# First expert stage in 64-slot units on quarters of the array; in both expert stages the last two units reach the tokens by one-hot products

## The chip, the cores and the metric

The kernel runs on one core of one Trainium2 chip. The metric is the device time of one execution in microseconds (us). The kernel before was run three times beside this work; the times were 405.24, 405.71 and 405.87, median 405.71.

## The reference, cut to what is computed

The input is 16 images of 96 x 96 pixels. A patch embedding (five shifted copies of each 16 x 16 patch, layer norm, linear map) gives 16 x 36 = 576 tokens of 192 numbers. Then follow an attention block with 12 heads and rounded operands, a first mixture of experts, a state-space block with a gated feed-forward part, and a second mixture of experts. Only the two mixtures of experts are changed.

```
# first mixture: 8 experts, the best one per token, hidden width 512
for e in range(8):
    mask = (max_ind == e)[:, None]
    xe = where(mask, x, 0)
    oe = silu(xe @ w1[e]) * (xe @ w2[e]) @ w3[e]
    out = out + where(mask, oe, 0)
out = out.astype(bfloat16) * max_prob          # then added to the residual stream

# second mixture: 8 experts, the best two per token, hidden width 768
# y = sum over the two experts of gate * (silu(x @ Wg[e].T) * (x @ Wu[e].T)) @ Wd[e].T
```

Everything is float32 except where the kernel names bf16.

## The kernel before, in words

576 tokens lie in SBUF as five tiles of 128 rows (`TT` = 5, the last has 64), 192 columns wide.

**Routing.** `experts(m, tile)` on DVE (m = 0 and 1 for the two mixtures) takes the largest logits, ranks each token within its expert, and gives each token and choice a slot. Slots are cut into units of 128 (`P`), each with one expert: units 0 to 7 are the first 128 slots of experts 0 to 7, the units from 8 on hold what is over. There are `M1_TILES` = 12 units in the first mixture and `M2_TILES` = 16 in the second, whatever the routing is. `src_id` (L1166) names the token of each slot, `row_id` (L1169) the DRAM row to which a slot's result goes.

**Data flow of a unit.** SP loads the expert's weights (`expert_weights`, L417 to L421: `wup` in four transfers, `wdn` in one) into one of 8 buffers (first mixture) or 6 (second). POOL gathers the unit's token rows from DRAM (`gather`, L597); for unit 0 PE does it by a product with a one-hot matrix (`first_tile`, L1547). PE transposes the rows (`gathered`, L1580), ACT and DVE copy them to `xgt` (L770, L1190). PE multiplies gate and up weights with the tokens: `up_main` (L1604) with the first 128 of 192 input rows on the whole array, `up_rest` (L1616) with the last 64, gate on rows 0 to 63 of the array and up on rows 64 to 127 at the same time. ACT takes silu (L774), DVE the product (L1196) to `ht`. PE multiplies by the down weights (`down`, L1629), ACT copies the result to `ysb` (L781), and POOL scatters it to the DRAM scratch `token_y` (L604). After the last unit SP waits for all scatters (`results`, L445) and loads `token_y` in token order to `yg` (L349). DVE adds gate times `yg` to the residual `h` (`routed`, L1211, in the first mixture; L1332 in the second, after which the tiles of `h` go out).

**Order.** Every engine's order is written out by hand. On PE, unit j is `up_main(j, 0)`, `up_main(j, 1)`, a transposition of a later unit, `up_rest(j, 0)`, `up_rest(j, 1)`, `down(j - 1)`. All weights go through SP's one queue, in program order: six loads of the first mixture after the embedding (`v_h` = 5), then the writes of the token rows (`token_rows`, L349), loads 6 and 7, loads from 8 on as buffers come free (`later_experts` waits for `p_y`, the count of finished `down`), then `results(0)`, then the first load of the second mixture. The loads of experts 0 to 7 of the first mixture have constant addresses, later ones take the expert's number from `te`.

**Layout of the weights in DRAM.** For the first mixture `w12` is, for each expert, 96 rows x 2 halves x 1024 columns (512 gate, 512 up) in float32; `w3` is 128 rows x 4 x 192. A unit's weights are 1.18 MB.

Of the kernel before, what the change touches and what calls it, by code (L numbers as in the profile page):

```python
# [50 lines left out]
M1_TILES = (T + E * (P - 1)) // P  # L51
# [5 lines left out]
W_LOADS = 5  # L57
AHEAD = 4
MAMBA_AT, ATTENTION_AT = 23 * 1024, 56 * 1024
# [38 lines left out]
def build(nc, A, out):  # L98

    with ExitStack() as ctx:  # L100
# [96 lines left out]
        slot_m = sb("slot_m", [P, 2, TT])  # L197
        slot_r = sb("slot_r", [P, 2, TT])
# [10 lines left out]
        def weight_buffers(m, n, hid):  # L209
# [60 lines left out]
        ysb = [sb("ysb0", [P, 2, D], BF16, scope=arena), sb("ysb1", [P, 2, D], scope=arena)]  # L270
        yg = [sb("yg0", [P, 1, TT, D], BF16, scope=arena), sb("yg1", [P, 2, TT, D], scope=arena)]
        xg = sb("xg", [P, M2_TILES, DW], scope=arena)
        xgt = sb("xgt", [P, 2, M2_TILES * P], scope=arena)
        one_first = sb("one_first", [P, TT, P], scope=arena)
        arena.close()
# [28 lines left out]
            d_gam d_x0 d_x0b d_w0b d_wub d_x1 d_x2 d_w0 d_w1 d_w2 d_wu d_att d_ssm d_tx d_out  # L304
# [5 lines left out]
            v_x2 v_fc v_cs v_f0 v_first v_val  # L310
            a_sq a_xp a_s12 a_std a_xt a_rx a_qf a_vf a_at a_of a_ot a_ex a_gt a_sg a_y a_cp a_z a_xs a_dt
            a_dec a_ysq a_fc a_f1
            p_ch p_st p_ht p_tr p_rt p_qk p_v p_sc p_av p_otr p_proj p_lg p_rk p_inv p_gt p_gu p_y p_in p_dt p_g
            p_seg p_xs p_ys p_ssq p_out p_fc p_f2""".split()}
        d_y = (S["d_ya"], S["d_yb"])
        MOE = (dict(n=M1_TILES, hid=M1_H, k=1, w12=A["m1_w12"], w3=A["m1_w3"], before=0, bufs=M1_BUFS),
               dict(n=M2_TILES, hid=M2_H, k=2, w12=A["m2_w12"], w3=A["m2_w3"], before=M1_TILES, bufs=M2_BUFS))
        for r in MOE:
            r["groups"] = [(0, 1), (1, 2)] + [(i, i + 2) for i in range(2, r["n"], 2)]
            r["group_of"] = [i for i, (lo, hi) in enumerate(r["groups"]) for _ in range(lo, hi)]  # L320
# [3 lines left out]
        def weight_uses(m, j):  # L324

            b = j % MOE[m]["bufs"]
            uses = j // MOE[m]["bufs"] + 1
            if m == 1:
                uses += len(range(b, M1_TILES, M1_BUFS))
            return b, uses  # L330

        def rows_gathered(m, i):
# [6 lines left out]
            return 16 * rows  # L339

# [6 lines left out]
        def _(sp):  # L347
# [56 lines left out]
            def expert_weights(m, j, e=None):  # L404
# [4 lines left out]
                b, _ = weight_uses(m, j)  # L409
# [7 lines left out]
                sp.dma_start(up[0:DH, 0:2 * hid], w12[:, 0, :]).then_inc(S[f"d_wb{b}"], 16)  # L417
                sp.dma_start(up[DH:P, 0:2 * hid], w12[0:lo, 1, :]).then_inc(S[f"d_wb{b}"], 16)
                sp.dma_start(up[0:REM, 2 * hid:3 * hid], w12[lo:DH, 1, 0:hid]).then_inc(S[f"d_wb{b}"], 16)
                sp.dma_start(up[REM:P, 2 * hid:3 * hid], w12[lo:DH, 1, hid:2 * hid]).then_inc(S[f"d_wb{b}"], 16)  # L420
# [31 lines left out]
            sp.wait_ge(S["v_h"], TT)  # L452
            for j in range(6):
                expert_weights(0, j)
# [20 lines left out]
            for t in range(TT):  # L475
                rows = P if t < TT - 1 else LAST
                sp.wait_ge(S["v_h"], 5 * TT + t + 1)
# [5 lines left out]
        def _(pool):  # L483
# [105 lines left out]
            def experts_io(m):  # L589
# [12 lines left out]
                def scatter(j):  # L602
                    pool.wait_ge(S["a_y"], j + 1 + before)
# [7 lines left out]
                for j in range(n):  # L611
# [3 lines left out]
                    if j >= 1:  # L615
                        scatter(j - 1)
                scatter(n - 1)
# [30 lines left out]
        def _(act):  # L648
# [94 lines left out]
            def experts(m):  # L743
# [22 lines left out]
                def gathered(i):  # L766

                    lo, hi = r["groups"][i]
                    act.wait_ge(S["p_gt"], 2 * (GROUPS[m] + i) + 1)
                    a.copy(xgt[:, 0, lo * P:hi * P], ps[:, 6, 0:(hi - lo) * P]).then_inc(S["a_gt"], 1)  # L770
# [5 lines left out]
                def result(j):  # L776

                    act.wait_ge(S["p_y"], j + (1 + before))
                    if j >= 2:
                        act.wait_ge(d_y[j % 2], j // 2 * 16 + 8 * before)  # L780
# [1064 lines left out]
```

## Time and profile before

| | |
|---|---|
| median of the runs | 405.71 us |
| profiled execution, its own time | 409.78 us |
| its span | 408.0 us |
| PE busy | 348.6 us (85%) |
| DVE, ACT, POOL busy | 184.0, 134.8, 104.5 us |
| moved by the DMA engines | 59.51 MB, mean 146 GB/s |

The span is the time from the first to the last instruction of the program in the profiled execution; its own time has some 1.8 us around it. A busy share is over the whole span. In the tables below a "x16" counts recorded instructions: a float32 product of the program is two MATMUL records (and two weight loads), a bf16 one is one. Times on the left are microseconds from the start of the span.

### The profile page before, as it was taken

How to read it: one execution, taken by the hardware profiler on the slowest of the kernel's cores; microseconds unless marked ns; L12 is line 12 of the kernel's file. 1: busy time of each engine (PE TensorE's matmuls, PEld its weight loads, DVE VectorE, ACT ScalarE, POOL GpSimd, SP SyncE). 2: the span in 40 equal slices, each digit the busy share in tenths (PEclk: the TensorE clock that was granted, in tenths of full speed). 3: DMA queues.
4: the chain of work that ended last, by engine and by line, in shares of the span. 5: the costliest groups of instructions: out<-in, count | busy, mean ns of one | idle time of the engine just before them, and what ended most of it. 6: DMA issues, size and time to landing. Idle time of an engine off the chain costs nothing.

```text
span 408.0 us, 7081 instructions
## 1 busy us (share of the span) xinstructions
PE 348.6 (85%) x2758; PEld 291.5 (71%) x2758; DVE 184.0 (45%) x474; ACT 134.8 (33%) x278; POOL 104.5 (26%) x133
## 2 busy tenths in 40 slices
PE   4999946989788999966896987888899999999970
PEld 1999923567667999962465654575799999999960
DVE  2786793996552222216398555266422212121213
ACT  2997311444303222321387042321321212121210
POOL 3299542000023443122032202000423232211120
PEclk9999976987776999996999798995999999999995
DMA  7933239930371795007003999002249999999204
GB/s 237 345 84 75 63 81 253 271 93 2 108 202 52 203 247 124 15 16 195 0 0 77 258 252 259 28 0 67 60 105 291 277 254 255 258 251 249 65 31 130
DMA packets 28707, 59.51 MB, mean 146 GB/s; under 512 B 10081, under 2 KB 15234, under 8 KB 28674
## 3 DMA queue, kind: packets, MB, share of 16 engines
q1 hardware_dynamic: 26274, 53.48, 50.1%
q0 software_dynamic: 2400, 5.57, 5.0%
q8 instruction: 22, 0.36, 0.4%
q14 instruction: 11, 0.09, 0.1%
HBM read 55.12 MB, written 3.92 MB: 145 GB/s over the span
## 4 chain that ended last, share of the span: by engine, by line
PE 60%; DVE 17%; ACT 8%; DMA 8%; issue 4%; SPq 2%; POOL 0%; DVEq 0%; POOLq 0%; ACTq 0%
PE ps L1604 15%; PE ps L1629 12%; PE ps L1616 9%; PE ps L1412 4%; PE ps L1345 4%; DMA xw<-in_xw 3%; DVE cv L1264 3%; ACT xp L661 2%; PE ps L1418 2%; DVE xn L974 2%; DVE xn L950 2%; PE ps L1467 2%; SPq L349 2%; PE ps L1547 2%; DMA yg<-token_y 2%
## 5 line engine op out<-in xcount | busy, mean ns | idle before, releaser
L1604 PE MATMUL ps<-xgt,wup 128*128 128x128 f32 x576 | 70.9, 280 | 2.3 <-DVE ht L1196 1.8
L1604 PEld LDWEIGHTS ps<-xgt,wup 128*128 128x128 f32 x576 | 69.4, 196 | 2.8 <-issue 2.8
L1196 DVE TENSOR_TENSOR ht<-sg,ps 128x384 f32<-128x384 f32 (+1 forms) x56 | 27.7, 497 | 77.5 <-ACT sg L774 75.5
L597 POOL DMA_INDIRECT xg<-token_x,src_id x26 | 25.3, 972 | 145.5 <-DVE src_id L1166 95.3
L1629 PE MATMUL ps<-wdn,ht 128*128 128x192 f32 x288 | 53.8, 335 | 0.0
L1345 PE MATMUL ps<-busy 128*128 128x512 bf16 x108 | 38.9, 486 | 11.1 <-DVE h L1211 6.6
L1629 PEld LDWEIGHTS ps<-wdn,ht 128*128 128x128 f32 x288 | 46.1, 190 | 3.1
L604 POOL DMA_INDIRECT token_y<-ysb,row_id x28 | 27.5, 981 | 67.6 <-ACT ysb L781 67.6
L774 ACT ACTIVATE sg<-ps 128x384 f32<-128x384 f32 (+1 forms) x56 | 24.8, 444 | 49.9 <-PE ps L1616 49.1
L1353 PE MATMUL ps<-weff,xp 128*128 128x193 f32 x240 | 39.9, 327 | 1.6 <-ACT xp L661 1.6
L1353 PEld LDWEIGHTS ps<-weff,xp 128*128 128x128 f32 x240 | 39.2, 190 | 2.4 <-issue 2.4
L1616 PE MATMUL ps<-xgt,wup 64*128 64x128 f32 x576 | 40.5, 286 | 0.0
L1616 PEld LDWEIGHTS ps<-xgt,wup 64*128 64x128 f32 x576 | 35.0, 190 | 4.2 <-issue 2.5
L1190 DVE COPY xgt<-ps 128x256 f32<-128x256 f32 (+1 forms) x14 | 5.7, 405 | 49.2 <-PE ps L1580 49.2
L1345 PEld LDWEIGHTS ps<-busy 128*128 128x128 bf16 x108 | 11.9, 116 | 22.2 <-issue 8.3
L661 ACT COPY xp<-xw 128x576 f32<-128x576 f32 x24 | 16.0, 667 | 6.7 <-DMA xw<-in_xw 6.7
L770 ACT COPY xgt<-ps 128x256 f32<-128x256 f32 (+1 forms) x14 | 5.0, 357 | 38.4 <-PE ps L1580 38.4
L1388 PE MATMUL ps<-ident,xn 128*128 128x128 f32 x30 | 6.3, 301 | 10.9 <-DVE xn L950 8.9
L690 ACT ACTIVATE std<-mv,eps_t 128x1 f32<-128x1 f32 x20 | 5.9, 294 | 28.4 <-DVE mv L960 28.4
L1388 PEld LDWEIGHTS ps<-ident,xn 128*128 128x128 f32 x30 | 3.9, 149 | 15.0 <-DVE xn L950 10.6
L781 ACT COPY ysb<-ps 128x192 f32<-128x192 f32 x16 | 5.1, 318 | 26.3 <-PE ps L1629 26.3
L909 DVE TENSOR_REDUCE acc<-wall 128x192 f32<-128x3072 f32 (+1 forms) x2 | 10.5, 5236 | 5.3 <-ACT wall L674 3.8
(295 smaller groups left out, 511.0 us busy)
## 6 DMA issues: line engine op xcount, KB each, us to landing
wup<-in_m_w SPq DMA_DIRECT2D x16, 576.0 KB, 8.5
wup<-in_m_w SPq DMA_DIRECT2D x48, 192.0 KB, 9.4
wdn<-in_m_w SPq DMA_DIRECT2D x16, 576.0 KB, 11.4
wup<-in_m_w SPq DMA_DIRECT2D x12, 384.0 KB, 6.1
wup<-in_m_w SPq DMA_DIRECT2D x36, 128.0 KB, 6.6
wdn<-in_m_w SPq DMA_DIRECT2D x12, 384.0 KB, 9.3
xw<-in_xw SPq DMA_DIRECT2D x2, 784.0 KB, 12.3
wall<-in_w_sh SPq DMA_DIRECT2D x2, 768.0 KB, 10.2
```

The costliest lines, as they stand in the source:

```text
L597: g.indirect_dma_start(xg[:, j, :], None, token_x[m], bass.IndirectOffsetOnAxis(ap=src_id[:, j:j + 1], axis=0))\
L604: g.indirect_dma_start(token_y[m], bass.IndirectOffsetOnAxis(ap=row_id[:, j:j + 1], axis=0), ysb[m][:, j % 2, :], None).then_inc(d_y[j % 2 ...
L661: a.copy(xp[:, n % RING, 0:T].rearrange("p (b r x) -> p b r x", r=GRID, x=GRID), img[:, :, wy:wy + GRID, wx:wx + GRID]).then_inc(S["a_xp"], 1)
L774: a.activation(sg[:, s, 0:half], ps[:, 2 * s, 0:half], ACT.Silu).then_inc(S["a_sg"], 1)
L1196: v.tensor_tensor(ht[:, j % 2, s, 0:half], sg[:, s, 0:half], ps[:, 2 * s + 1, 0:half], ALU.mult)\
L1264: v.scalar_tensor_tensor(out=cv[:, r], in0=xpad[:, r, :, k:k + NTOK], scalar=convw[:, r, k:k + 1], in1=cv[:, r], op0=ALU.mult, op1=ALU.add ...
L1345: mm(ps[:, bank, :], busy[:, 0:P], busy[:], start=True, stop=True)
L1353: return mm(ps[:, TILE_BANK[t], 0:D + 1], xp[:, n % RING, t * P:t * P + P], weff[:, n, 0:D + 1], start=(n == 0), stop=(n == NCH - 1))
L1412: mm(outs[v][b], w[:, 0, c0:c1], moving(v, b), start=True, stop=False)
L1604: mm(ps[:, 2 * s + g, c * P:c * P + P], up[:, col:col + P], xgt[:, 0, j * P:j * P + P], start=(c == 0), stop=False)
L1616: ins = mm(ps[:, 2 * s + g, c * P:c * P + P], up[rows, col:col + P], xgt[rows, 1, j * P:j * P + P], start=False, stop=(c == tiles - 1))
L1629: ins = mm(ps[:, 4 + j % 2, 0:D], ht[:, j % 2, c // tiles, c % tiles * P:c % tiles * P + P], dn[:, c, :], start=(c == 0), stop=(c == 2 * t ...
```

## The change

**Units of 64 slots.** In the first mixture slots are cut into units of 64 (`H`): 16 of them (`M1_HALVES`), two by two in 8 pairs (`M1_TILES` = 8). Each half has its own expert and so its own weights. A pair is gathered by one indirect transfer as before. The 192 input rows are now three blocks of 64 (`KB` = 3), and each product is done on a quarter of the array: 64 rows x 64 columns of it, gate on rows 0 to 63, up on rows 64 to 127, and two column halves i. `across`, `up_half` and `down_pair` take the place of `gathered`, `up_main`/`up_rest` and `down`. The pair's result is the sum of two PSUM banks: ACT copies one to `y_low`, DVE adds the other (`both_rows`). On PE the order is `up_half(j, 0)`, `down_pair(j - 1)`, `across(j + 1)`, `up_half(j, 1)`.

**Weight layout and loads.** `wup` holds for each block k both the gate rows (partitions 0 to 63) and the up rows (64 to 127), 512 columns each. A load is seven transfers instead of five: blocks 0 and 2 by one transfer each, whose destination is 128 partitions x 512 and whose source is 2 (gate, up) x 64 rows x 512; block 1 by four of 32 rows; and `wdn`. There are 16 loads instead of 12.

**The last two units.** In both mixtures the last two units (`KEPT` = 2) are not scattered. `token_y` is filled with zeros by three transfers on SP ahead of the first weight load. DVE makes one-hot matrices, tokens x slots, for the two units (`last_units`, after units 2 and 3, and 4 and 9; in the second mixture they carry the gates), PE transposes them (`kept_across`) with the last units, ACT and DVE copy them out, and after the last `down` PE adds one-hot times result for each token tile (`combine`). In the first mixture `combine` also takes `yg` through an identity product and DVE's `routed` reads PSUM; in the second, DVE adds the PSUM tile to `h` after both `yg` parts. `results` waits for the scatters of the other units alone.

```diff
-M1_TILES = (T + E * (P - 1)) // P
+H = 64
+M1_HALVES = (T + E * (H - 1)) // H
+M1_TILES = (M1_HALVES + 1) // 2
+KB = D // H
-W_LOADS = 5
+W_LOADS = (7, 5)
+KEPT = 2
...
+        KEPT_AFTER = ((2, 3), (4, 9))
...  SP: expert_weights
+                if m == 0:
+                    def both(k):
+                        return up[:, k * hid:(k + 1) * hid]
+
+                    def gate_and_up(half, rows):
+                        return w12[rows, half, :].rearrange("p (g n) -> g p n", g=2)
+
+                    pieces = [(both(0), gate_and_up(0, slice(0, H))), (both(2), gate_and_up(1, slice(lo, DH)))]
+                    for g in range(2):
+                        at = H * g
+                        pieces += [(up[at:at + DH - H, hid:2 * hid], w12[H:DH, 0, g * hid:(g + 1) * hid]),
+                                   (up[at + DH - H:at + H, hid:2 * hid], w12[0:lo, 1, g * hid:(g + 1) * hid])]
...
+                for dst, src in pieces:
+                    sp.dma_start(dst, src).then_inc(S[f"d_wb{b}"], 16)
                 sp.dma_start(down[:], w3).then_inc(S[f"d_wb{b}"], 16)
...  SP: later_experts
-                for j in range(first, r["n"]):
+                for j in range(first, M1_HALVES if m == 0 else r["n"]):
                     if j == E:
                         sp.wait_ge(S["v_te"], m + 1)
-                    sp.wait_ge(S["p_y"], j - r["bufs"] + 1 + r["before"])
+                    last = j - r["bufs"]
+                    sp.wait_ge(S["p_y"], (last // 2 if m == 0 else last) + 1 + r["before"])
...  SP: results
-                    sp.wait_ge(d_y[b], 8 * (r["n"] + r["before"]))
+                    sp.wait_ge(d_y[b], 8 * (r["n"] - KEPT) + scattered(m))
...  SP, after v_h = 5
+            zeros = (busy[:, 0:D], busy[:].bitcast(F32)[:, 0:D])
+            for m in range(2):
+                for k in range(MOE[m]["k"]):
+                    y = token_y[m][k * TPAD:(k + 1) * TPAD, :].rearrange("(t p) d -> p t d", p=P)
+                    load(y, zeros[m].unsqueeze(1).broadcast_to([P, TT, D]), "d_zero")
...  POOL: experts_io
-                    if j >= 1:
+                    if j == 0:
+                        pool.wait_ge(S["d_zero"], 48)
+                    elif j <= n - KEPT:
                         scatter(j - 1)
-                scatter(n - 1)
...  DVE: last_units(l), both_rows(j)
+                    v.tensor_tensor(ysb[m][:, j % 2, :], y_low[:], ps[:, 5, 0:D], ALU.add).then_inc(S["v_y"], 1)
...
+                    for k in range(K):
+                        for t in range(TT):
+                            ...
+                                ins = v.tensor_scalar(one_last[m][:, l, k, t, :], pos_r[:], slot_k[:, l, k, t:t + 1],
+                                                      gate[:, k, t:t + 1], ALU.is_equal, ALU.mult)
...  PE: first_tile
+                        if m_ == 0:
+                            for c in range(KB):
+                                for i in range(2):
+                                    ins = mm(ps[H * i:H * i + H, 6, c * P:c * P + P], xn[0:k, t, H * c:H * c + H],
+                                             one_first[0:k, t, :], start=(t == 0 and c == 0),
+                                             stop=(t == TT - 1 and c == KB - 1))
...  PE
+                def across(j):
+                    ...
+                    for c in range(KB):
+                        for s in range(2):
+                            rows = slice(H * s, H * s + H)
+                            for i in range(2):
+                                ins = mm(ps[H * i:H * i + H, 6 + s, c * H:c * H + H], xg[rows, j, H * c:H * c + H],
+                                         ident[rows, rows], start=True, stop=True)
+                def up_half(j, s):
+                    ...
+                    for c in range(hid // P):
+                        for k in range(KB):
+                            for g in range(2):
+                                rows = slice(H * g, H * g + H)
+                                for i in range(2):
+                                    col = c * P + H * i
+                                    ins = mm(ps[H * i:H * i + H, 2 * s + g, c * H:c * H + H], up[rows, k, col:col + H],
+                                             xh[rows, t, k, :], start=(k == 0), stop=(k == KB - 1))
+                def down_pair(j):
+                    ...
+                    for c in range(hid // P):
+                        for g in range(2):
+                            rows = slice(H * g, H * g + H)
+                            for i in range(2):
+                                dn = wbuf[0][(2 * j + i) % M1_BUFS][1]
+                                ins = mm(ps[H * i:H * i + H, 4 + g, 0:D], ht[rows, j % 2, i, c * H:c * H + H],
+                                         dn[rows, c, :], start=(c == 0), stop=(c == hid // P - 1))
+                def kept_across(l):
+                    ...
+                    for t in range(TT):
+                        ...
+                        ins = nc.tensor.transpose(at, one_last[1][0:k, l, 0, t, :], ident[0:k, 0:k])
+                def combine():
+                    pe.wait_ge(S["a_oh"], 1 if m_ == 0 else 1 + KEPT)
+                    pe.wait_ge(S["v_oh2"], 1 if m_ == 0 else 1 + KEPT)
+                    pe.wait_ge(S["v_y" if m_ == 0 else "a_y"], n)
+                    if m_ == 0:
+                        pe.wait_ge(S["d_yg"], 32)
+                    for t in range(TT):
+                        k = P if t < TT - 1 else LAST
+                        o = ps[0:k, TILE_BANK[t], 0:D]
+                        if m_ == 0:
+                            mm(o, identb[0:k, 0:k], yg[0][0:k, 0, t, :], start=True, stop=False)
+                        for l in range(KEPT):
+                            ins = mm(o, kept_at[m_][:, l, t * P:t * P + k], ysb[m_][:, (n - KEPT + l) % 2, :],
+                                     start=(m_ == 1 and l == 0), stop=(l == KEPT - 1))
+                        ins.then_inc(S["p_cmb"], 1)
```

## Rows read from the trace of the kernel before

**Rows 1.** The page's chain that ended last: shares of the span by line.
```profile
PE ps L1604 15%; PE ps L1629 12%; PE ps L1616 9%; PE ps L1412 4%; PE ps L1345 4%; DMA xw<-in_xw 3%; DVE cv L1264 3%; ACT xp L661 2%; PE ps L1418 2%; DVE xn L974 2%; DVE xn L950 2%; PE ps L1467 2%; SPq L349 2%; PE ps L1547 2%; DMA yg<-token_y 2%
```
**Rows 2.** The chain in order of time, first mixture: start us, us, what.
```profile
114.69 3.75 PE ps L1547 x20
...
119.51 3.75 DMA xg<-token_x,src_id
...
126.24 3.75 PE ps L1604 x16
129.99 0.85 PE ps L1580 x4
130.84 1.09 PE ps L1616 x16
131.94 1.50 PE ps L1629 x8
133.43 1.78 PE ps L1604 x16
...
177.42 2.81 PE ps L1629 x16
```
**Rows 3.** Timeline, end of the first mixture: start us, us, engine line op, tiles, shapes, count.
```profile
180.25 0.32 ACT L781 CAST ysb<-ps 128x192 bf16<-128x192 f32 x1 [0.98 <-PE ps L1629]
180.84 0.97 POOL L604 DMA_INDIRECT token_y<-ysb,row_id  x1 [0.33 <-ACT ysb L781]
183.12 0.96 SPq L349 DMA_DIRECT2D yg<-token_y  x2
186.35 0.42 DVE L1211 SCALAR_TENSOR_TENSOR h<-yg,gate,h 128x192 f32<-128x192 bf16 x1 [8.05 <-DMA yg<-token_y]
```
**Rows 4.** Stretches: window us; length; busy us (instructions) by engine; PEclk; DMA share; GB/s.
```profile
9.00:16.00 7.00, 6.40 (x39) 6.43 (x40) 4.93 (x6) 7.00 (x14) 0.00 (x0) 1.00 1.03 426
60.00:86.00 26.00, 19.07 (x122) 11.35 (x123) 18.62 (x33) 6.53 (x8) 3.89 (x5) 0.82 1.00 252
126.20:129.90 3.70, 3.66 (x17) 3.69 (x18) 0.29 (x1) 0.00 (x0) 0.94 (x1) 0.50 0.12 35
135.00:157.00 22.00, 22.00 (x203) 20.70 (x203) 5.05 (x12) 6.17 (x17) 9.08 (x11) 1.00 0.99 246
```
**Rows 5.** SP's queue: the first transfer of all, first and last of a later load.
```profile
56.77 0.33 SPq L417 DMA_DIRECT2D wup<-in_m_w  x1
...
134.52 0.34 SPq L417 DMA_DIRECT2D wup<-in_m_w  x1
...
136.94 0.45 SPq L421 DMA_DIRECT2D wdn<-in_m_w  x1
```
**Rows 6.** Groups of instructions by shape: busy us, mean ns of one, idle us before.
```profile
L774 ACT ACTIVATE sg<-ps 128x256 f32<-128x256 f32 x24 | 9.2, 383 | 16.2 <-PE ps L1616 15.4
L1196 DVE TENSOR_TENSOR ht<-sg,ps 128x256 f32<-128x256 f32 x24 | 10.1, 420 | 26.2 <-ACT sg L774 25.9
L1140 DVE TENSOR_SCALAR one_first<-pos_r,slotf 128x128 f32<-128x128 bf16 x10 | 2.1, 281 | 0.1
L1321 DVE TENSOR_TENSOR h<-ps,hb 128x192 f32<-128x192 f32 x5 | 1.7, 340 | 1.4 <-PE ps L1759 1.4
```
**Rows 7.** Timeline, products on two column halves in the state-space block.
```profile
231.11 1.35 PE L1712 MATMUL ps<-mix,dtx 128*64 128x72 f32 x36
```
**Rows 8.** Timeline, end of the kernel.
```profile
390.73 4.17 PE L1629 MATMUL ps<-wdn,ht 128*128 128x192 f32 x24
394.94 0.32 ACT L781 COPY ysb<-ps 128x192 f32<-128x192 f32 x1 [1.63 <-PE ps L1629]
...
397.92 2.15 SPq L349 DMA_DIRECT2D yg<-token_y  x4
403.43 1.73 DVE L1332 SCALAR_TENSOR_TENSOR h<-yg,gate,h 128x192 f32<-128x192 f32 x5 [0.36 <-DMA yg<-token_y]
403.88 2.37 SPq L349 DMA_DIRECT2D out_h<-h  x5
```

More of the change, by code:

```diff
@@ L322, in build, with weight_loads @@
         RESTS = [0, len(MOE[0]["groups"]) - 1]
-        def weight_uses(m, j):
+        def weight_loads(m, j):
             b = j % MOE[m]["bufs"]
-            uses = j // MOE[m]["bufs"] + 1
+            loads = W_LOADS[m] * (j // MOE[m]["bufs"] + 1)
             if m == 1:
-                uses += len(range(b, M1_TILES, M1_BUFS))
-            return b, uses
+                loads += W_LOADS[0] * len(range(b, M1_HALVES, M1_BUFS))
+            return b, 16 * loads
         def rows_gathered(m, i):
@@ L339, in rows_gathered, with scattered @@
             return 16 * rows
+        def scattered(m):
+            return 8 * (M1_TILES - KEPT) if m == 1 else 0
         N_ATT, N_SSM, N_FIRST = 16 * 26, 16 * 40, 14
@@ L602, in scatter @@
                 def scatter(j):
-                    pool.wait_ge(S["a_y"], j + 1 + before)
+                    pool.wait_ge(S["v_y" if m == 0 else "a_y"], j + 1)
                     g.indirect_dma_start(
@@ L778, in result @@
                     act.wait_ge(S["p_y"], j + (1 + before))
+                    if m == 0:
+                        if j >= 1:
+                            act.wait_ge(S["v_y"], j)
+                        a.copy(y_low[:], ps[:, 4, 0:D]).then_inc(S["a_yh"], 1)
+                        return
                     if j >= 2:
-                        act.wait_ge(d_y[j % 2], j // 2 * 16 + 8 * before)
+                        act.wait_ge(d_y[j % 2], j // 2 * 16 + scattered(m))
                     a.copy(ysb[m][:, j % 2, :], ps[:, 4 + j % 2, 0:D]).then_inc(S["a_y"], 1)
@@ L1076, in experts @@
                 r = MOE[m]
-                n, half, before, K = r["n"], r["hid"] // 2, r["before"], r["k"]
+                n, half, before, K, L = r["n"], r["hid"] // 2, r["before"], r["k"], r["slots"]
+                over = (M1_HALVES if m == 0 else n) - E
                 i_ln = 2 if m == 0 else 5
@@ L1334, in _ @@
                                            op0=ALU.mult, op1=ALU.add).then_inc(S["v_h"], 1)
+            for t in range(TT):
+                rows = P if t < TT - 1 else LAST
+                dve.wait_ge(S["p_cmb"], TT + t + 1)
+                dve.wait_ge(S["v_h"], 5 * TT + t + 1)
+                v.tensor_tensor(h[0:rows, t, :], h[0:rows, t, :], ps[0:rows, TILE_BANK[t], 0:D], ALU.add)\
+                    .then_inc(S["v_h"], 1)
         @block.tensor
@@ new lines, in down_pair @@
+                def down_pair(j):
+                    pe.wait_ge(S["v_ht"], 2 * j + 2)
+                    if j >= 1:
+                        pe.wait_ge(S["a_yh"], j)
+                        pe.wait_ge(S["v_y"], j)
+                    else:
+                        pe.wait_ge(S["v_id"], 1)
+                    for c in range(hid // P):
+                        for g in range(2):
+                            rows = slice(H * g, H * g + H)
+                            for i in range(2):
+                                dn = wbuf[0][(2 * j + i) % M1_BUFS][1]
+                                ins = mm(ps[H * i:H * i + H, 4 + g, 0:D], ht[rows, j % 2, i, c * H:c * H + H],
+                                         dn[rows, c, :], start=(c == 0), stop=(c == hid // P - 1))
+                    ins.then_inc(S["p_y"], 1)
@@ new lines, in experts @@
+                if m_ == 0:
+                    for j in range(n):
+                        up_half(j, 0)
+                        if j >= 1:
+                            down_pair(j - 1)
+                        if j + 1 < n:
+                            across(j + 1)
+                        else:
+                            for l in range(KEPT):
+                                kept_across(l)
+                        up_half(j, 1)
+                    down_pair(n - 1)
+                    combine()
+                    return
@@ L1644, in experts @@
                 down(n - 1)
+                combine()
             experts(0)
```

196 lines of the change are left out of this document (153 added, 43 removed).

## The prediction

> **What bounds the kernel now.** I read the page's chain first, then the same chain in order of time, then the stretches with their DMA rate. Matmuls of the two mixtures of experts are the three longest entries of the chain [rows 1]: there PE waits for nothing, and what is taken off it is time won, as long as nothing else is late. In the first mixture a unit of 128 slots costs PE 1.78 us (16 records, L1604) + 1.09 (L1616) + 1.50 (L1629), and 0.85/2 or less for the transpositions (0.85 at half clock), some 4.6 us in all [rows 2]. Twelve of them end at 180.2. Then comes a tail without PE: copy (180.25), scatter (180.84), load of `yg` (183.12), and DVE's first add at 186.35 [rows 3]. The same tail stands at the end: ACT copies at 394.94, DVE's last add ends at 405.16, the last store is issued by 406.25 and the span ends at 408.0 [rows 8]. The weights are hidden today, but not by much: from 135 to 157 four loads keep the DMA engines 0.99 busy at 246 GB/s [rows 4].
>
> **PE's work in the first mixture.** An `up_half` has 4 x 3 x 2 x 2 = 48 products, 96 records, four quarters at a time: 24 rounds of 64 columns. A record of 128 columns takes 1.78/16 = 0.111 us at full clock and 3.75/16 = 0.234 at half [rows 2], where the granted clock is 0.50, 1.2 GHz [rows 4]; for 64 columns half of that. So an `up_half` is 1.3 us, or 2.8 at half clock. `down_pair` has 8 rounds of 192 columns at 1.50/8 = 0.19: 1.5 us (3.0). `across` is 6 rounds: 0.3. A pair costs 2 x 1.3 + 1.5 + 0.3 = 4.5 us, eight of them 36 where twelve units took 55. That four quarters run together no row shows. Two row halves do: 16 records of 128 columns in 1.09 us, 0.068 each instead of 0.111 [rows 2]. Two column halves do: 36 records of 72 columns in 1.35 us, 0.037 each, where one after the other would have 0.111 x 72/128 = 0.062 [rows 7]. The bounds for a pair are 4.5 us and, with two quarters at a time, 9.
>
> A rule of the Trainium skill speaks against this: a matmul with few columns costs as much as one with 60, the overhead is paid per instruction (TensorEngine Tiling (Array Packing), Performance Considerations, Instruction Overhead). By it, in an estimate of mine with its 60 cycles at 2.4 GHz, 25 ns, for each of a pair's 216 records of 64 columns, a pair would be 5.4 + 1.5 = 6.9 us. The row with two column halves stays above that at 37 ns, so it can't refute it; the sum below doesn't change by it, since weights are later than that.
>
> **The beginning.** `first_tile` has 60 records, 30 rounds, instead of 20 (3.75 us, L1547): +1.8 us before the first gather, 119.5 becomes 121.3 [rows 2]. No wait of later units hangs on it if the loads set the pace.
>
> **The loads.** This is the term that decides. A load has 1.18 MB, as before; 16 instead of 12. SP issues seven transfers instead of five; five take 134.52 to 137.39, 0.58 us each [rows 5], so seven 4.1 us: no bound below. The two large ones (262,144 bytes each) have a destination of 128 rows and a source of 2 x 64 rows. All large transfers of the kernel before have 96, 32, 64 or 128 rows outermost on both sides, all multiples of 16, so the trace doesn't show what an outermost 2 does. The bounds: over all 16 engines at 252 GB/s [rows 4] such a piece is 1.0 us; over two engines each has 131,072 bytes. One engine moves 252/16 = 15.8 GB/s when all are busy, 426/16 = 26.6 at best [rows 4]: 8.3 to 4.9 us a piece. I take two engines. The work has to be dealt out along a dimension that both sides count, and the outermost ones are 128 and 2; nothing else of the two matches. The Trainium skill says it outright: the number of engines is the largest up to 16 that divides the outermost dimension of both sides (DMA: Bandwidth & Descriptors, Why a DMA increments its semaphore by 16 and not by 1). No row here shows it; by it the piece has two engines.
>
> The two busy engines then carry for each load 2 x 131,072 bytes and 1/16 of the other 655,360: 303,104 bytes. Of the rate I take 24 GB/s, near the upper row, since fourteen engines are idle beside them, and below it for rows of 2 KB: 12.6 us a load. In order of the queue: SP starts at 56.8 [rows 5]. The zeros are 1.23 MB, 4.9 us at 252 GB/s: 61.7. Sixteen loads: 202 us. Token rows, gathers and scatters are 1.9 MB, their share of the two engines 117,000 bytes, 4.9 us. With 1 us to land the last load is there at 269.6. The queue is never empty between: loads 0 to 7 last until 61.7 + 101 = 163, and load 8 waits only for the first `down_pair`. That comes late too: the token rows stand behind loads 0 to 5 on the same engines (61.7 + 76 = 137), so the first gather lands at 142 instead of 123, and the first pair is done by 152.
>
> **The tail of the first mixture.** PE has idled for most of 12 us before each half, so I count half clock: last `up_half` 2.8, silu and product 0.38 + 0.42 [rows 6] with 0.1 of handing over, `down_pair` 3.0, copy to `y_low` 0.32 [rows 3], sum 0.35, handing over 0.2, three bf16 products and handing over 0.8: 8.4 us (5.3 at full clock). `yg` is issued after the sixth scatter, stands behind the loads in the queue and lands 1 us after the last: hidden. `routed(0)` starts at 278.0, not 186.35: +91.7 us. One-hot matrices of DVE (5 x 0.28 and a few small ones, 1.6 us twice) lie in that waiting. What follows is DVE's chain as before, so it moves along rigidly; the first load of the second mixture is early.
>
> **The second mixture.** PE gets ten float32 transpositions with units 14 and 15: 20 records at 0.11, +2.2 us, no cover. DVE's `last_units` is 10 x 0.28 + 0.9 + 0.2 = 3.9 us after units 4 and 9; DVE is busy 1.2 us of a unit's 6.4, and its next product is asked for some 5 us later: hidden; without that cover up to 2 x 2.7. The tail after the last `down` (394.90) is now: copy 0.35, then `combine`, 20 records at 0.17 (4.17/24 [rows 8]) and handing over, 3.6, last add 0.34 [rows 6], then issue, landing and end, 2.84 as before (408.0 - 405.16): 7.1 instead of 13.1, less 0.4 because PE's pace spreads the five stores: 6.7. The 14th scatter is issued before `down(14)`, its load of `yg` (2.15 + 3.4 us) and the ten adds are done 1 us before `combine` needs DVE. So -6.4 + 2.2 = -4.2 us. Bounds: 0 if `yg` is late by a unit, -6.
>
> **Sum.** In the profiled execution: 409.78 + 91.7 - 4.2 = 497.3 (span 495.5). That execution was 4.1 us above the median of the runs; from the median: 405.7 + 87.5 = 493.2.
>
> **Rivals.** *A. The two pieces are spread over 16 engines.* For it: every other transfer is. Then two loads, a gather and a scatter, 2.54 MB, take 10.3 us at 246 GB/s [rows 4], more than PE's 4.5, so the loads bound pairs 4 to 7. The first `down_pair` ends near 132 (before 133.4, [rows 2]), load 8 starts at 134.1, eight are there at 175.4, the tail is 5.3 to 8.4: `routed(0)` at 182.3, -4.1. Time 405.7 - 4.1 - 4.2 = 397.4. Faster: this is the case of the other sign. *B. Sixteen engines, but quarters don't overlap fourfold.* A pair costs 9 us; eight from 122 on (half an `up_half` runs before the first gather is there at 124) and a tail of 5 end at 199, +12.7 - 4.2: 414. The first mixture gets slower from 7.4 us a pair, (186.35 - 5 - 122)/8, the kernel from 7.9. Against it: both halvings overlap. *C. Two engines, and slow ones*, at the 15.8 GB/s of a full queue: a load 19.2 us, +105: 599. Against it: that rate was shared by sixteen. *D. Two engines at 26.6 GB/s*: 11.4 us, -19: 474.
>
> **Numbers.** Two engines 0.79 (C at its end 0.03, D beside the forecast), A 0.15, B 0.04, else 0.02. The likeliest case alone has 465 to 545. For the range I go to A, as without it 0.2 would be left: 394 to 545. About 0.2% (0.8 us) is what a measurement of this kernel can tell from no change. Faster: A but for a little of it, 0.15. Same 0.02. Slower: two engines and B, 0.83.
>
> **What would show it.** Landing of the first pieces: 5 us or more apart and DMA busy share near 0.13 to 0.2 through the first mixture, PE idle before `up_half` on `wup`, one load every 12 to 13 us. `combine` without `yg` on its wait. Clock 0.50 in the last halves. The prediction is wrong if the DMA share is near 1.0 there and loads come every 5 us; then A holds.

## The result, and the profile after

The changed kernel takes 493.62 us (median of 4 runs, 492.27 to 494.69) against 405.79 us for the kernel before (4 runs); the ratio is 1.2153, with a 95% interval of 1.2105 to 1.2202. The forecast was 493.2. The profiled execution took 494.69 us and has a span of 493.0.

The page of the kernel after, first the slices, then the chain by engine and by line (its line numbers are the changed kernel's: L454 issues the pieces of the first weights, L455 the second weights, L1803 is `up_half`, L1822 `down_pair`, L1779 `across`, L1864 the one-hot products):

```profile
PE   6999388976026742323252888788879999999996
DMA  7832332232433323233227000799010399999703
...
PE 39%; SPq 26%; DMA 10%; DVE 10%; ACT 5%; issue 5%; POOL 4%; DVEq 0%; ACTq 0%; POOLq 0%
SPq L454 24%; PE ps L1739 8%; PE ps L1764 7%; DMA wdn<-in_m_w 6%; PE ps L1751 5%; PE ps L1803 4%; DVE cv L1385 3%; PE ps L1539 2%; DMA token_x<-xn 2%; PE ps L1822 2%; DMA xg<-token_x,src_id 2%; DVE xn L1042 1%; PE ps L1472 1%; PE ps L1965 1%; PE ps L1545 1%
...
L1803 PE MATMUL ps<-xgt,wup 64*64 64x64 f32 x1536 | 38.8, 281 | 69.8 <-DMA wdn<-in_m_w 66.8
```

Where [rows 1] had matmuls of the two mixtures on top, SP's queue now has 24% of the span, and `up_half` has waited 66.8 us for weights. The chain in order of time (start, us, what) shows one load of SP's queue, then the first pair of units:

```profile
90.67 0.54 SPq L454
91.25 3.95 SPq L454
95.25 5.06 SPq L454
100.35 0.42 SPq L454
...
101.74 0.42 SPq L455
102.21 0.54 SPq L454
...
127.58 9.82 DMA token_x<-xn
...
138.27 6.39 DMA xg<-token_x,src_id
144.71 0.92 PE ps L1779 x24
145.63 4.04 PE ps L1803 x192
149.66 1.50 PE ps L1822 x29
...
151.94 1.51 PE ps L1803 x102
153.45 1.90 issue
155.35 1.54 PE ps L1803 x89
```

From 90.67 to 102.21 is one load. Its plain transfers are issued in 0.42 us each; each of the two large pieces keeps a place in SP's queue for 4 to 5 us. What the DMA engines do meanwhile stands in three stretches (window; length; busy us of PE, PEld, DVE, ACT, POOL; PEclk; DMA share; GB/s); in the first a large piece is alone under way:

```profile
70.50:75.00 4.50, 4.50 (x33) 3.60 (x32) 3.61 (x9) 1.43 (x2) 0.00 (x0) 1.00 0.13 51
64.00:126.00 62.00, 49.52 (x583) 35.69 (x583) 37.16 (x130) 19.80 (x35) 0.00 (x0) 0.86 0.29 97
156.00:256.00 100.00, 38.33 (x1316) 35.78 (x1312) 9.67 (x33) 7.39 (x21) 6.28 (x7) 0.63 0.31 101
```

A share of 0.13 is 2.1 of 16 engines, so two engines at 51/2 = 25.5 GB/s each; [rows 4] had 0.99 and 246 GB/s. The last load and the tail, beside [rows 3]:

```profile
256.44 11.01 DMA wdn<-in_m_w
267.45 0.04 issue
267.49 2.88 PE ps L1803 x96
...
270.81 0.43 DVE ht L1269
...
271.28 1.57 PE ps L1822 x32
...
273.84 0.24 PE ps L1862
...
274.29 0.43 DVE h L1332
```

The first add of the first mixture is at 274.29 instead of 186.35: +87.9 us. From there to the end of the span it is 218.7 us instead of 221.7, in these two executions. The end of the kernel, beside [rows 8], in the timeline:

```profile
485.55 0.32 ACT L830 COPY ysb<-ps 128x192 f32<-128x192 f32 x1 [1.63 <-PE ps L1764]
486.01 3.63 PE L1864 MATMUL ps<-ysb,kept 128*128 128x192 f32 x20 [0.50 <-ACT ysb L830]
487.45 3.13 SPq L368 DMA_DIRECT2D out_h<-h  x5
489.69 0.35 DVE L1460 TENSOR_TENSOR h<-h,ps 64x192 f32<-64x192 f32 x1 [0.44 <-PE ps L1864]
```

The loads of `yg` are off this path. From the last copy to the end of the span it is 7.5 us, where before it was 408.0 - 394.94 = 13.1.

### The profile page after: what moved, and what is told of

It reads as the page before. It is cut to its first block, busy times and chain, and to the rows that moved or that the text cites. A ratio compares the mean times of both kernels' runs of the same rounds, so it can differ in the third digit from the quotient of the medians.

```text
span 493.0 us, 10359 instructions
## 1 busy us (share of the span) xinstructions
PE 349.3 (71%) x4311; PEld 291.4 (59%) x4311; DVE 194.6 (39%) x519; ACT 132.1 (27%) x269; POOL 93.2 (19%) x121
## 4 chain that ended last, share of the span: by engine, by line
PE 39%; SPq 26%; DMA 10%; DVE 10%; ACT 5%; issue 5%; POOL 4%; DVEq 0%; ACTq 0%; POOLq 0%
SPq L454 24%; PE ps L1739 8%; PE ps L1764 7%; DMA wdn<-in_m_w 6%; PE ps L1751 5%; PE ps L1803 4%; DVE cv L1385 3%; PE ps L1539 2%; DMA token_x<-xn 2%; PE ps L1822 2%; DMA xg<-token_x,src_id 2%; DVE xn L1042 1%; PE ps L1472 1%; PE ps L1965 1%; PE ps L1545 1%
## 5 line engine op out<-in xcount | busy, mean ns | idle before, releaser
L1803 PE MATMUL ps<-xgt,wup 64*64 64x64 f32 x1536 | 38.8, 281 | 69.8 <-DMA wdn<-in_m_w 66.8
L1269 DVE TENSOR_TENSOR ht<-sg,ps 128x384 f32<-128x384 f32 (+1 forms) x48 | 24.4, 509 | 140.6 <-ACT sg L818 138.9
L1803 PEld LDWEIGHTS ps<-xgt,wup 64*64 64x64 f32 x1536 | 36.5, 192 | 71.4 <-DMA wdn<-in_m_w 68.0
L1739 PE MATMUL ps<-xgt,wup 128*128 128x128 f32 x384 | 45.6, 275 | 1.2 <-DVE ht L1269 1.2
L1739 PEld LDWEIGHTS ps<-xgt,wup 128*128 128x128 f32 x384 | 44.8, 192 | 1.4 <-issue 1.4
L644 POOL DMA_INDIRECT token_y<-ysb,row_id x20 | 19.7, 986 | 102.0 <-DVE ysb L1277 63.6
L1764 PE MATMUL ps<-wdn,ht 128*128 128x192 f32 x192 | 35.2, 334 | 0.0
L1764 PEld LDWEIGHTS ps<-wdn,ht 128*128 128x128 f32 x192 | 30.8, 190 | 1.8
L1751 PE MATMUL ps<-xgt,wup 64*128 64x128 f32 x384 | 25.8, 280 | 0.0
L1779 PE MATMUL ps<-ident,xg 64*64 64x64 f32 x168 | 4.5, 234 | 28.4 <-DMA xg<-token_x,src_id 25.6
L1751 PEld LDWEIGHTS ps<-xgt,wup 64*128 64x128 f32 x384 | 22.8, 188 | 2.1 <-issue 1.3
L1779 PEld LDWEIGHTS ps<-ident,xg 64*64 64x64 f32 x168 | 4.2, 146 | 29.2 <-DMA xg<-token_x,src_id 25.7
L1822 PE MATMUL ps<-wdn,ht 64*64 64x192 f32 x256 | 15.6, 390 | 1.0 <-DVE ht L1269 1.0
```

The source lines that it names most:

```text
L644: g.indirect_dma_start(token_y[m], bass.IndirectOffsetOnAxis(ap=row_id[:, j:j + 1], axis=0), ysb[m][:, j % 2, :], None).then_inc(d_y[j % 2 ...
L1269: v.tensor_tensor(ht[:, j % 2, s, 0:half], sg[:, s, 0:half], ps[:, 2 * s + 1, 0:half], ALU.mult)\
L1739: mm(ps[:, 2 * s + g, c * P:c * P + P], up[:, col:col + P], xgt[:, 0, j * P:j * P + P], start=(c == 0), stop=False)
L1751: ins = mm(ps[:, 2 * s + g, c * P:c * P + P], up[rows, col:col + P], xgt[rows, 1, j * P:j * P + P], start=False, stop=(c == tiles - 1))
L1764: ins = mm(ps[:, 4 + j % 2, 0:D], ht[:, j % 2, c // tiles, c % tiles * P:c % tiles * P + P], dn[:, c, :], start=(c == 0), stop=(c == 2 * t ...
L1803: ins = mm(ps[H * i:H * i + H, 2 * s + g, c * H:c * H + H], up[rows, k, col:col + H], xh[rows, t, k, :], start=(k == 0), stop=(k == KB - 1))
```

## The experiments

Times are medians, to be compared with the kernel before on the same chip: 405.8 us for e1 to e4, 405.5 for e5 to e8, 406.9 for e9 to e11. "2 outermost" says that the slowest dimension of a transfer's source has two entries (gate, up), each of 64 rows. "Issue" in a row of waits is time in which an engine stood still and nothing in the profile released it.

**e1_plain: the two pieces as four transfers of 64 rows.**

```diff
-pieces = [(both(0), gate_and_up(0, slice(0, H))), (both(2), gate_and_up(1, slice(lo, DH)))]
+for k, half, rows in ((0, 0, slice(0, H)), (2, 1, slice(lo, DH))):
+    for g in range(2):
+        pieces.append((both(k)[H * g:H * g + H], w12[rows, half, g * hid:(g + 1) * hid]))
```

> Edit: each of the two large pieces of a load goes as two transfers of 64 rows (gate columns, up columns), nine transfers a load, same bytes, everything else as in the changed kernel. Theory T (a piece whose source has 2 outermost and whose destination has 128 rows runs on two DMA engines, and the busier engines' bytes, 303,104 a load at 24.6 GB/s, set 12.3 us a load): now all transfers have 32 or 64 rows on both sides, 1.18 MB a load over sixteen engines, 4.8 us at 246 GB/s; the first add of the first mixture near 182, second mixture 3.0 us shorter than before as measured, time 405.8 - 4.1 - 3.0 = 399 (397 to 402; nine issues of 0.46 us each are 4.1 us a load and set nothing). Rival S (what costs is the issuing of many rows by SP, 4.6 to 5.1 us for a piece of 128 rows, whatever the engines): 128 rows of 2 KB are still issued per piece, so a load keeps its 12.3 us and the time stays at 494.

Measured: 411.8 us (409.99 to 419.35), ratio to before 1.0155 (1.004 to 1.027). The same bytes into the same places, and 82 us are gone: rival S falls. But 399 was expected; 12.8 us are missing. The waits of PE from 118 to 192 us (us in total, times, longest), then SP's timeline (start, us):

```profile
PE ps L1806 <- issue: 10.2, 6, 2.4
PE ps L1806 <- DMA wdn<-in_m_w: 7.9, 3, 4.1
PE ps L1782 <- issue: 5.3, 4, 2.0
```
```profile
155.68 5.10 SPq L457 DMA_DIRECT2D wup<-in_m_w  x8
160.96 0.35 SPq L458 DMA_DIRECT2D wdn<-in_m_w  x1
162.08 1.28 SPq L457 DMA_DIRECT2D wup<-in_m_w  x2
```

Two things show. A load whose address comes from a register takes 162.08 - 155.68 = 6.4 us on SP with nine transfers, more than the 4.8 us in which its data would move at 246 GB/s [rows 4]: SP sets the pace of loads 8 to 15. And PE stands still for 15.5 us ("issue") with nothing to release it. e5_five and the runs behind it part these.

**e2_half: only the second piece in plain transfers.** The edit is that of e1_plain for `both(2)` alone.

> Edit: only the second large piece of a load goes as two transfers of 64 rows; the first stays in one with 2 outermost. Theory T: the busier engines carry 131,072 + 917,504/16 = 188,416 bytes a load, at 24.6 GB/s 7.7 us; sixteen loads are 16 x 4.6 = 74 us shorter, time 420. A half dose gives a little more than half the effect left, 14 us above the kernel before. Rival S, a hold of 5 us for each transfer with 2 outermost whatever its bytes: 5 + 7 x 0.46 = 8.2 us a load, 428. Rival S by rows: 494.

Measured: 432.2 us (2 runs), ratio 1.066 (1.0535 to 1.0785). Loads with fixed addresses came 8.4 us apart (7.7 expected), the one piece held SP 4.7 us. The time is 12 us over T's sum, as in e1_plain. The dose shows, but this run alone doesn't choose between T and a hold of 5 us for each such transfer: that rival's 8.2 us a load and 428 are the nearer numbers. The next run chooses.

**e3_cols: each piece in two column halves, still 2 outermost.**

```diff
+pieces.append((both(k)[:, at], gate_and_up(half, rows)[:, :, at]))   # at: 256 of 512 columns
```

> Edit: both large pieces keep 2 outermost in the source, but each goes as two transfers of half the columns (128 rows of 1 KB): nine transfers, same bytes on the same two engines, twice the number of rows. Theory T: 12.3 us a load as before, 494, and up to 510 if rows of 1 KB move at less than 24.6 GB/s on an engine; each SP issue is held about 2.5 us instead of 5. Rival S (5 us for each such transfer or for each 128 rows): 4 x 5 + 5 x 0.46 = 22.3 us a load, 16 x 10 = 160 us more, 654.

Measured: 496.3 us (2 runs). Twice the transfers and rows, 2.6 us of SP's queue each, 12.7 us a load. The hold goes with the bytes, not with the number of transfers or rows. That leaves no form of S: 654 was its time here. A stretch with one such piece alone:

```profile
73.00:75.00 2.00, 2.00 (x16) 1.47 (x14) 1.97 (x5) 0.20 (x1) 0.00 (x0) 1.00 0.13 48
```

**e4_four: the same pieces with 4 outermost.**

```diff
+return w12[REM // 2 * k:REM // 2 * (k + 1)].rearrange("p m (g n) -> (m g) p n", g=2)
```

> Edit: the same seven transfers and bytes, but the two large pieces read with 4 outermost (32 rows of w12 each) instead of 2; the rows then stand in another order, so that the first mixture computes with other weights. Theory T: four engines carry a piece, 2 x 65,536 + 655,360/16 = 172,032 bytes a load on the busiest, 7.0 us; 16 x 5.3 = 85 us less than the changed kernel, time 409, and the busy share of the DMA engines while one piece is alone under way is 0.25 instead of 0.13. Rival: any piece whose two sides differ in their outermost number runs on two engines, or is held 5 us at issue whatever the number: 494.

Measured: 423.1 us (2 runs), loads 7.3 us apart (7.0 expected), 2.4 us of SP's queue for a piece, and with one alone under way:

```profile
71.40:73.70 2.30, 2.30 (x18) 1.85 (x17) 2.26 (x6) 0.57 (x1) 0.00 (x0) 1.00 0.26 102
```

Twice the share and twice the rate of 2 outermost. In both cases, with 128 on the other side, the number of engines is the outermost number of the source. The time is 14 us over a sum that knows only bytes.

**e5_five: a load in five transfers.**

```diff
+chunks = up.rearrange("p (k n) -> p k n", k=KB)
+pieces.append((chunks[at:at + H // 2], w12[:, i, g * hid:(g + 1) * hid].rearrange("(p k) n -> p k n", k=KB)))
+# the tokens' columns to match: x.rearrange("r (n k) -> r k n", k=KB)[:, c]
```

> Edit: a load in five transfers (gate and up columns, each in two of 32 rows x 3 chunks x 2 KB, and the second weights), for which the three chunks of the contraction take every third row of w12 and every third column of the tokens; same bytes, products and instructions of PE. In the run with nine plain transfers SP took 6.7 us for a load whose address comes from a register, and was never waiting after 129 us, and PE stood still for 15.5 us between 118 and 192 in ten stretches that nothing in the profile releases, each beside a fetch of 16 KB of PE's own instructions. Theory F (PE's instructions are supplied no faster than one such block of 256 in 4.3 us; a pair has 248 matmuls and as many weight loads, 496, so 8.3 to 8.5 us): SP's load falls to 4.4 us, but the pairs keep their 8.5 us; the first down_pair ends at 128, the eighth at 187.6, the first add 189, time 405.8 + 2.9 - 3.0 = 406 (403 to 408). Rival P (only SP's issues held the pairs; PE needs its 5.0 us busy a pair): loads of 5.15 us set the end, first add 177 to 184, time 394 to 400.

Measured: 420.5 us (418.31 to 423.44), ratio 1.0371 (1.0303 to 1.0438). Both theories missed, on the high side, and the kernel is slower than e1_plain, although SP needs less time for a load. PE stood still ("issue") for 26 us and never waited for weights. Its timeline, and two stretches of this run:

```profile
155.81 3.08 PE L1803 MATMUL ps<-xgt,wup 64*64 64x64 f32 x110
164.20 2.10 PE L1803 MATMUL ps<-xgt,wup 64*64 64x64 f32 x69 [5.31 <-issue]
```
```profile
150.00:166.00 16.00, 7.98 (x240) 7.59 (x236) 2.54 (x10) 1.38 (x4) 0.99 (x1) 0.71 1.06 230
182.00:197.00 15.00, 10.74 (x495) 10.10 (x490) 2.51 (x7) 2.73 (x8) 1.94 (x2) 0.95 0.09 22
```

With the DMA engines full PE runs 476 instructions (matmuls and weight loads) in 16 us, with the engines nearly idle 985 in 15; it stands still for 8.0 us of the first stretch and 4.3 of the second. The trace's queue for instructions moves 16 KB at a time. While weights were moved such packets started at 145.62, 152.54, 161.40, 170.12 and 176.54, 6.4 to 8.9 us apart; from 182.03 to 196.78, with the engines nearly idle, 3.4 to 3.9 us apart. The page counts 34 such packets here and 22 in the kernel before:

```profile
q8 instruction: 34, 0.56, 0.6%
```

So theory F's pace, one block in 4.3 us whatever the transfers, is wrong. What it says PE waits for is tested by e7_wide, e9_light and e10_third. The Trainium skill says that crossing such a block is "mostly hidden" (Runtime: NRT & Kernel Launch, Instruction fetch mechanics); in this stage of 64-column products the trace disagrees: PE stood still for 15.5 us in e1_plain and 26 us here.

Waiting isn't what makes this run slower than e1_plain. Between the ends of the first and the eighth `down_pair`, e1_plain (first row) and this run (second):

```profile
128.00:190.00 62.00, 37.64 (x1627) 34.60 (x1625) 12.34 (x39) 9.78 (x27) 7.88 (x8) 0.92 0.64 185
136.00:203.70 67.70, 43.90 (x1622) 40.74 (x1616) 12.18 (x39) 9.76 (x27) 7.88 (x8) 0.85 0.75 175
```

PE stood still for 24.4 and 23.8 us, about the same (in e1_plain 7.9 of it for weights). The 5.7 us between them are PE's work, 43.9 us for 37.6, at a mean granted clock of 0.85 for 0.92. The other 8 us by which the first add is later (205.14 for 191.55) lie before the first `down_pair` ends; what caused them no run shows.

**e6_rows: 64 rows x 128 columns as the stationary.**

```diff
-for i in range(2):
-    ins = mm(ps[H * i:H * i + H, 2 * s + g, c * H:c * H + H], up[rows, k, col:col + H], ...)
+ins = mm(ps[:, 2 * s + g, c * H:c * H + H], up[rows, k, c * P:c * P + P], ...)
```

> Edit: the run with five transfers a load, and up_half's products with a stationary of 64 rows x 128 columns instead of two of 64 x 64: the same sums in the same banks, two running together instead of four, 48 matmuls an up_half instead of 96. Theory F: a pair has 304 instructions instead of 496, 5.1 us by supply, PE's array time stays 5.0; now the loads of 5.15 us bound pairs 4 to 7: the last has landed near 170, a tail of 5.4 to 8.8, first add 176 to 179, time 405.8 - 8.9 - 3.0 = 394 (391 to 398). Rival P: no gain over the run with five transfers, both at 394 to 400. Rival Q (four quarters overlap, two halves overlap less): a pair gets up to 2.6 us longer than with quarters, and the time is above that of the run with five transfers.

Measured: 428.1 us (413.76 to 431.68; the six runs spread too far for an interval). By time nothing is decided: the median is above e5_five, as rival Q has it, the fastest run is below it, and all are above the 398 of theory F. What Q says of the pair, up to 2.6 us longer, the trace bears out. The instructions did fall, to 28 packets (6 fewer, for 768 fewer matmuls and weight loads each: 256 instructions in a packet), and PE's "issue" fell from 26 to 8 us, but its work grew:

```profile
148.78 5.58 PE L1801 MATMUL ps<-xgt,wup 64*128 64x64 f32 x96
```

Two `up_half` in 5.58 us, 2.8 each at clock 0.99, where quarters take 1.5. Halves of 128 stationary columns with 64 moving ones take 0.058 us a record, two at a time; quarters 0.0156. The spread goes with the clock: the fastest run had a mean granted clock of 0.921, the slowest 0.883. In the profiled run two of the eight pairs took 10.1 and 10.4 us for their two `up_half` instead of 5.6, at a granted clock of some 0.50; why the clock fell in one run more than in another is open.

**e7_wide: twice the columns in `down_pair`.** Moving operand `dn[rows, c, :].unsqueeze(1).broadcast_to([H, 2, D])`.

> Edit: the run with five transfers, with down_pair's products over twice the columns (the 192 columns of the second weights twice, 384 into the bank), same number of instructions: PE has 1.5 us more work a pair. Theory F: PE's stretches without instructions shrink by it, the pairs keep 8.5 us, the time stays within 2 us of the run with five transfers (406 by F). Rival P: 8 x 1.5 = 12 us more where PE bounds the pairs, 6 to 12 where the loads do in half of them.

Measured: 422.3 us (2 runs), 1.8 us more than e5_five, while `down_pair` took 2.8 us instead of 1.5 (8 x 1.3 = 10 us more work); PE's "issue" fell from 26 to 17 us, and the first add came at 206.31 instead of 205.14. The added work went into time in which PE had stood still: PE's work isn't what bounds the stage, as theory F has it.

**e9_light: late loads without their first weights.**

```diff
+if j >= M1_BUFS:
+    pieces = []
```

> Edit: the run with five transfers a load, but loads 8 to 15 of the first mixture fetch their second weights only (393,216 bytes instead of 1.18 MB; up_half of these units computes with the first weights of units 0 to 7). PE's instructions are the same. In the run with five transfers PE's blocks of 256 instructions came 8.8 us apart while the DMA engines were busy (152.54, 161.40, 170.12; share 1.06) and 3.7 us apart when they were idle (182.03 to 196.78 in four; share 0.07). Theory F2 (PE waits for its instructions, and their fetches stand behind the weights): a pair of 496 instructions costs 1.94 x 3.7 = 7.2 us, seven pairs 50 us after the first down_pair's end at 136: first add 188 instead of 205, time 403 (400 to 407). Rival F (blocks at 4.3 us whatever the transfers): seven pairs 58 us, 411. Rival P (PE's 5.0 us of work): 387. Rival, the late loads and not the fetches were the wait: below 395.

Measured: 407.6 us (402.82 to 410.04, 8 runs), just above F2's range (400 to 407); first add at 187.95 (188 expected), and between 135 and 180 us eleven blocks of instructions, 4.1 us apart (3.7 expected). PE's instructions were not touched, and e5_five had no wait for weights that could have gone; only other transfers went, and the first add came 17.2 us earlier. The same stretch as above, to the end of this run's eighth `down_pair`:

```profile
136.00:186.60 50.60, 37.59 (x1583) 34.04 (x1573) 11.85 (x38) 9.25 (x27) 7.85 (x8) 0.97 0.41 110
```

It is 17.1 us shorter than e5_five's: 10.8 us less standing still (13.0 for 23.8), and 6.3 us less of PE's own work at a granted clock of 0.97 instead of 0.85. So the transfers cost PE more than the wait for instructions: the clock was lower too in the run in which it stood still more.

**e10_third: one third of `up_half` left out of that kernel.**

> Edit: the run with light late loads, and up_half without the middle chunk of the contraction: 64 matmuls instead of 96, a pair has 184 matmuls and 368 instructions instead of 496; PE's own work falls by 1.0 us a pair. Theory F2: a pair costs 368/256 x 3.7 = 5.3 us instead of 7.2, first add 13 us earlier than with all chunks, time 390 (387 to 394). Rival (the pace is set by PE's work and the hand-overs with ACT and DVE, with the instructions arriving in time): 8 x 1.0 = 8 us or less, time 395 or above.

Measured: 397.6 us (2 runs), which is the rival's "395 or above" and not F2's 387 to 394; first add at 177.90, 10.0 us earlier, between the two (13 expected, 8 or less by the rival). From 136.0 to 176.5, where the eighth `down_pair` ends, PE worked 33.1 us instead of 37.6 and stood still for 7.5 instead of 13.0: fewer instructions did shorten the wait for them. But the blocks came 4.3 us apart and not 3.7, so that F2's fixed pace fails here; that PE's own work shares the bound is argued, not shown.

**e8_tail: the one-hot products of the second mixture alone, on the kernel before.** `kept_across`, `last_units`, `combine` as in the change, for m = 1; twelve 128-slot units stay.

> Edit: the kernel before, its first mixture untouched, with the one-hot products for the last two units of the second mixture alone; the two zero fills of that mixture's result rows (983 KB) are issued behind its first weight load. The changed kernel's second mixture and all behind it was 3.0 us shorter than before (first add to end 218.7 instead of 221.7 us). Theory: this part is worth the same alone, 405.8 - 3.0 = 402.8 (401.5 to 404.5). Rival: the 3.0 us come from something else in the changed kernel (another clock after the long idle time, another place of the loads), and alone the part is worth 0 to 1 us: 405 to 406.

Measured: 401.3 us (398.96 to 403.58, 6 runs), ratio 0.9895 (0.9847 to 0.9943), 4.3 us (2.3 to 6.2). The rival (405 to 406) falls; the 3.0 us of the theory lie in the interval, and the median is just below its range. A part may be the clock, whose mean over the runs was 0.931 here and 0.925 in the kernel before. Among the eleven runs of that kernel 0.01 of clock went with some 1 us, which would make it 0.6 us, an estimate.

**e11_both: the one-hot products of both mixtures, on the kernel before.** The same for m = 0, and its zero fill ahead of the weights.

> Edit: the kernel before with its 128-slot units, and the last two units of both mixtures taken to the tokens by one-hot products: the whole of the change but the 64-slot tiles. The run with the second mixture alone had 401.3. In the first mixture the tail from the last copy (180.25) to the first add (186.35) becomes copy 0.32, hand-over 0.25, three bf16 products and hand-over 0.45, 1.1 us instead of 6.1; PE gets ten bf16 transpositions without cover, 1.0 us; the zero fill of 246 KB stands ahead of the weights, 1 us, hidden. Theory: 4.0 us less, 397.3 (395.5 to 399). Rival (the load of the other rows, issued only when the tenth scatter has landed, is late for the sum, or the fills delay the first gather): 0 to 2 us less, 399.5 to 401.5.

Measured: 398.4 us (395.06 to 399.05, 6 runs), in the theory's range and below the rival's. It is faster than either kernel: 8.5 us below the kernel before by the medians, 9.8 us (8.0 to 11.5) by the ratio of 0.976 (0.9717 to 0.9803). The mean granted clock was 0.936 here and 0.921 in the kernel before, by the same estimate 1.4 us of it. The end of the first mixture, beside [rows 3]:

```profile
179.39 0.32 ACT L797 CAST ysb<-ps 128x192 bf16<-128x192 f32 x1 [0.98 <-PE ps L1686]
179.97 0.24 PE L1719 MATMUL ps<-yg,identb 128*128 128x192 bf16 x1 [0.61 <-ACT ysb L797]
180.41 0.42 DVE L1262 SCALAR_TENSOR_TENSOR h<-ps,gate,h 128x192 f32<-128x192 f32 x1 [2.97 <-PE ps L1721]
```

1.0 us from the last copy to the first add, where e8_tail (176.23 to 182.90) has 6.7.

## Why the prediction was right, step by step

- **Two engines for a piece: right**, and now shown by share (0.13, and 0.26 with 4 outermost) and by e1_plain. The reason given was argued from the two sides' outermost numbers. The rule of the Trainium skill named there (DMA: Bandwidth & Descriptors, Why a DMA increments its semaphore by 16 and not by 1) gives two engines for 2 and four for 4, and these traces agree.
- **24 GB/s on the busy engines, 12.6 us a load: right.** Measured 12.3, 303,104/12.3 = 24.6 GB/s. That term, taken sixteen times, carries the result: the last load is there at 267.45 (269.6).
- **Token rows, gather, first pair:** 137.4 (137), 144.7 (142; a gather on these engines costs 6.4 us, not 3.75), 151.2 (152).
- **SP's issue "no bound": wrong in form.** Each piece holds the queue as long as it moves, 9.7 of a load's 12.3 us, so the chain names SP. The sum doesn't change, as the same bytes set both; the sign to look for was the hold at issue, since most of the landings can't be read from the trace.
- **DMA share 0.13 to 0.2: too low.** It was 0.29 to 0.31: the other 655,360 bytes of a load add a share of 0.16 to 0.18. PE's wait named `wdn`, the last transfer of a load, not `wup`.
- **PE's sizes:** `up_half` 1.5 us (1.3) and 2.88 at half clock (2.8), `across` 0.5 (0.3), `down_pair` 1.5 (1.5). A pair is 5.0 us busy, not 4.5. The Trainium skill's rule of some 60 cycles for each matmul (TensorEngine Tiling (Array Packing), Performance Considerations, Instruction Overhead), paid by one record after the other, would make an `up_half` 96 x 25 ns = 2.4 us, an estimate; the trace has 1.5 us, 15.6 ns a record with four quarters at a time, and disagrees.
- **Tail of the first mixture 8.4 us: 6.8.** The last `up_half` ran at half clock, as forecast (2.88 us, clock 0.50). The last `down_pair` ran in 1.57 us at full clock, where 3.0 had been counted.
- **Second mixture -4.2: -3.0** in the profiled execution, -4.3 (-6.2 to -2.3) by e8_tail. The end gave 5.6 us of the 6.4 (13.1 to 7.5). The ten transpositions are ten records, not twenty, and cost 0.54 us for each of the two units (L1846 starts at 472.36, the next products at 472.90), 1.1 us for 2.2. Between the first add and the last copy it took 211.3 us for 208.6; 1.6 us of these 2.7 are not explained.
- **The total:** +87.9 - 3.0 = +84.9 us of span (+91.7 - 4.2 = +87.5 forecast), 493.0 for 495.5. In time it was 493.6 for 493.2, and that closeness is luck. The parts were 2.5 us too high. The profiled execution before, from which they were counted, was 4.1 us above its median, the one after only 1.1 above.
- **Rival A's 397.4, which had a chance of 0.15, was a wrong sum.** Had the pieces been spread, the time would have been 412 to 420 (e1_plain, e5_five): slower. The step that failed is "more than PE's 4.5, so the loads bound". A pair of 64-slot units has 496 instructions, where two units of 128 slots have some 168 (2 x 42 matmuls and as many weight loads, [rows 2]), and e7_wide, e9_light and e10_third show that they don't arrive in time; in e1_plain SP's issues bound as well, 6.4 us a load. No sum here counted instructions. The 64-slot tiles lose with every layout of the loads tried here (the fastest, e1_plain, has 411.8 us with the one-hot products in it); the one-hot products alone win 8.5 to 9.8 us.

What stays open: how much of the 64-slot stage could be won with few transfers and fewer instructions at once; whether the fetches wait in the same engines' queues behind the weights or for memory (e9_light shows that the other transfers delay them, not where); and what sets the 3.7 us of a block when the DMA engines are nearly idle, the fetch itself or the pace at which PE takes its instructions.

## What to carry to other kernels

Before two transfers are merged into one by splitting off a small outermost dimension, read that number on both sides: here, with 2 or 4 against 128, the smaller one was the number of DMA engines that worked on it. When a change cuts the array into smaller tiles, count PE's instructions in a stage as well as its columns, and hold them against the rate at which blocks of 256 came while the DMA engines were busy (here 6.4 to 8.9 us; 3.4 to 3.9 us with nearly idle engines). And price the parts of a change one by one: here a gain of some 9 us stood inside a net loss of 88.

## What the hardware showed that was not expected

- A transfer of 262,144 bytes on two engines keeps SP's queue for 4 to 5 us, on four for 2.4, a plain one of 65,536 or 393,216 bytes for 0.42: an issue is not free where its engines are few.
- PE's instructions come in blocks of 16 KB over the DMA engines, and a stage that consumes them quickly slows while weights are moved: without two thirds of the late loads' bytes (e9_light) PE stood still for 10.8 us less than in e5_five.
- With nine transfers, a load with its address in a register took 6.4 us on SP (e1_plain, 155.68 to 162.08), one with a fixed address 4.9 us (63.48 to 68.39).
- Products of 64 moving columns on 64 x 64 quarters, four at a time, cost 0.0156 us a record, on 64 x 128 halves, two at a time, 0.058.
